# Products of value and output weights kept in DRAM in the first half of a latent attention, and loaded by GpSimd's queue in the second half

## The reference

```python
ctx_c = jnp.einsum('bhsl,bld->bhsd', attn, kv_r)          # probabilities by latent rows, 128 wide
ctx_lat = jnp.einsum('bhsd,hkd->bhsk', ctx_c, w_kc_kv)    # value weights of each of 16 heads
ctx = ctx_lat.transpose(0, 2, 1, 3).reshape(Bv, Sv, H * K)
return ctx @ Wo.T                                         # output weights
# outside:  x = x + jnp.tanh(g_xattn[0]) * that
```

```python
scale = jnp.mean(jnp.abs(w)) + EPS
wq = jnp.clip(jnp.round(w / scale), -1.0, 1.0)
```

## Time and profile before

| | us |
|---|---|
| median of three runs (2047.39 to 2053.69) | 2050.95 |
| the profiled execution's own time | 2053.51 |
| its span | 2051.8 |
| TensorE busy | 1848.8 (90%) |
| VectorE busy | 1403.8 (68%) |
| ScalarE busy | 975.6 (48%) |
| GpSimd busy | 680.5 (33%) |

### The profile page before, as it was taken

How to read it: one execution, slowest core, us unless ns; L and a number is a source line. 1 busy time by engine, 2 the same in 40 slices (tenths; PEclk the granted TensorE clock), 3 DMA queues, 4 the chain that set the end, 5 groups by cost and what they waited for, 6 DMA issues and landing times. The chain is left out here.

```text
span 2051.8 us, 31294 instructions
## 1 busy us (share of the span) xinstructions
PE 1848.8 (90%) x11258; PEld 1452.6 (71%) x11258; DVE 1403.8 (68%) x2821; ACT 975.6 (48%) x2042; POOL 680.5 (33%) x628
## 2 busy tenths in 40 slices
PE   4899999999999899998978997999758899999996
PEld 4677887777877677766754444666537889999996
DVE  5776677777678777788767883766636436666664
ACT  3444444433444344443445654555343236666663
POOL 4332122333523312233100131332221554665653
PEclk9999999999999999999989997999879999999999
DMA  5022201220311322122133111000040447877873
GB/s 201 16 84 81 83 23 61 84 88 3 114 38 35 126 92 75 33 80 96 39 125 151 46 38 32 1 1 1 1 160 23 150 89 211 243 242 228 241 240 76
DMA packets 52397, 192.38 MB, mean 94 GB/s; under 512 B 7678, under 2 KB 11902, under 8 KB 41494
## 3 DMA queue, kind: packets, MB, share of 16 engines
q1 hardware_dynamic: 40550, 167.01, 23.1%
q0 software_dynamic: 11408, 23.37, 6.2%
q10 hardware_dynamic: 288, 0.00, 0.0%
HBM read 156.99 MB, written 33.36 MB: 93 GB/s over the span
## 5 line engine op out<-in xcount | busy, mean ns | idle before, releaser
L363 POOL TENSOR_TENSOR la_q_roped<-la_q_roped 128x400 f32<-128x400 f32 x128 | 139.4, 1111 | 685.8 <-DVE la_q_roped L819 685.8
L722 ACT ACTIVATE la_probs<-banks,la_minus_max 100x361 f32<-100x361 f32 x256 | 144.7, 565 | 197.3 <-DVE la_minus_max L909 197.3
L819 DVE TENSOR_TENSOR la_q_roped<-banks,la_rope_q 128x400 f32<-128x400 f32 x384 | 196.8, 564 | 26.2 <-PE banks L490 16.5
L2069 DVE TENSOR_TENSOR ex_weights_low<-ex_raw_weights,ex_weights_high 128x2048 fp32r<-128x2048 f32 x60 | 137.6, 2293 | 54.9 <-ACT ex_weights_high L1964 52.1
L527 PEld LDWEIGHTS banks<-identity,la_probs 100*121 100x121 f32 x768 | 113.3, 185 | 73.4 <-DVE la_probs L916 48.0
L916 DVE TENSOR_SCALAR la_probs<-la_probs,la_rsum 100x361 f32<-100x361 f32 x256 | 154.5, 603 | 9.1
L538 PE MATMUL banks<-la_probs_t,la_kv_rows 121*128 121x200 f32 x768 | 151.4, 333 | 0.0
L527 PE MATMUL banks<-identity,la_probs 100*121 100x100 f32 x768 | 126.3, 273 | 23.3 <-DVE la_probs L916 20.1
L909 DVE TENSOR_REDUCE la_minus_max<-banks 100x1 f32<-100x361 f32 x256 | 134.8, 527 | 17.1 <-PE banks L518 10.3
L2336 POOL TENSOR_TENSOR ex_g_low<-ex_g,ex_g_high 128x256 fp32r<-128x256 f32 (+1 forms) x104 | 86.7, 950 | 177.4 <-ACT ex_g_high L2008 176.9
L1964 ACT CAST ex_weights_high<-ex_raw_weights 128x2048 fp32r<-128x2048 f32 x60 | 114.1, 1902 | 42.2 <-PE banks L2417 33.9
(11 more groups left out here) (335 smaller groups left out, 5300.7 us busy)
## 6 DMA issues: line engine op xcount, KB each, us to landing
ex_raw_weights<-w_exp SPq DMA_DIRECT2D x60, 1024.0 KB
la_weights<-w_pack SPq DMA_DIRECT2D x15, 1856.0 KB, 7.7
la_kv_turned<-w_ffn SPq DMA_DIRECT2D x30, 384.0 KB
la_rope_k<-w_ffn SPq DMA_DIRECT2D x30, 384.0 KB
qf_sign_weights<-ffn_signs SPq DMA_DIRECT2D x3, 2048.0 KB, 10.0
ffn_signs<-la_ffn_signs SPq DMA_DIRECT2D x30, 192.0 KB, 2.1
residual<-x SPq DMA_DIRECT2D x2, 2048.0 KB, 14.9
out<-ex_block_out POOLq DMA_DIRECT2D x13, 256.0 KB, 4.3
```

The source lines that it names most:

```text
L363: pool.tensor_tensor(roped[:, h, 0, c, :], roped[:, h, 0, c, :], roped[:, h, 1, 1 - c, :], ALU.add).then_inc(b_add, 1)
L722: act.activation(prob[:, s % 4, 0:L], ps[0:S, s % 2, 0:L], ACT.Exp, bias=nmax[:, s % 4:s % 4 + 1], accum_out=sums[:, s % 4:s % 4 + 1]).the ...
L819: dve.tensor_tensor(roped[:, h, v, c, :].rearrange("p (b s) -> p b s", b=GB), ps[:, B_BANKS[k % 2], 0:NT].rearrange("p (b s) -> p b s", b=GB),
L2069: dve.tensor_tensor(wl[:, m, :], raw[:, m, :], wh[:, m, :].bitcast(F32), ALU.subtract).then_inc(w_low[m], 1)
```

## The change

In the first half, SyncE stores `mh` and `ml` of each pass to a DRAM tensor (`keep`, 512 KB each). In the second half, `wout` on TensorE, `wout_high` on ScalarE and `wout_low` on VectorE are left out; GpSimd's queue loads the two matrices instead (`bring`) once the last `out` of the pass before is done, and the first `out` of a pass waits for them.

```diff
@@ latent_attention
+    kept_m = nc.dram_tensor("wout_parts", (PAIRS, 2, DC, 2 * D), F32).ap()
@@ SyncE
+                def keep(n):
+                    sp.wait_ge(m_low, 2 * n + 2)
+                    for i, m in enumerate((mh, ml)):
+                        sp.dma_start(kept_m[n, i], m[:].rearrange("p h d -> p (h d)").bitcast(F32)).then_inc(m_out, 16)
+
                 for n in range(2, RUNS + 1):
+                    if n <= PAIRS + 1:
+                        keep(n - 2)
                     refill_sums(n - 1)
                     refill_signs(n - 2, slice(3, None))
@@ GpSimd
+                def bring(n):
+                    pool.wait_ge(m_out, 32 * PAIRS)
+                    pool.wait_ge(o_psum, n * HB)
+                    for i, m in enumerate((mh, ml)):
+                        pool.dma_start(m[:].rearrange("p h d -> p (h d)"),
+                                       kept_m[n - PAIRS, i].bitcast(F32R)).then_inc(m_in, 16)
@@
                     if starts_half(n):
                         rotate(1, range(HB))
+                    if n >= PAIRS:
+                        bring(n)
                     for u in range(UNITS):
                         partners(n, u)
@@ TensorE, mix and out
-                    else:
+                    elif n < PAIRS:
                         pe.wait_ge(m_low, n * 2 + 1)
@@
-                    if b == 0:
+                    if b == 0 and n < PAIRS:
                         pe.wait_ge(m_low, n * 2 + 2)
+                    elif b == 0:
+                        pe.wait_ge(m_in, 32 * (n - PAIRS + 1))
@@ TensorE, pair
-                    wout(n, 0)
+                    if n < PAIRS:
+                        wout(n, 0)
                     absorb(n, 0)
                     widen(n, 3, 0)
-                    wout(n, 1)
+                    if n < PAIRS:
+                        wout(n, 1)
@@ ScalarE
                     act.wait_ge(m_psum, n * 2 + h + 1)
+                    if n:
+                        act.wait_ge(m_out, 32 * n)
@@ ScalarE, pair
-                    wout_high(n, 0)
+                    if n < PAIRS:
+                        wout_high(n, 0)
@@
-                        if s == 0:
+                        if s == 0 and n < PAIRS:
                             wout_high(n, 1)
@@ VectorE, pair
-                        if s in (MIX - 2, MIX - 1):
+                        if s in (MIX - 2, MIX - 1) and n < PAIRS:
                             wout_low(n, s - MIX + 2)
```

More of the change, by code:

```diff
@@ L212, in latent_attention @@
         m_psum, m_high, m_low = sem("wout_psum"), sem("wout_high"), sem("wout_low")
+        m_out, m_in = sem("wout_stored"), sem("wout_loaded")
         a_psum, a_high, a_low = sem("q_psum"), sem("q_high"), sem("q_low")
```

## The result

The changed kernel takes 2057.15 us (median of 7 runs, 2054.03 to 2059.57) against 2048.79 us for the kernel before in the same runs: 8.4 us more by the medians. The ratio of the means is 1.0035, with a 95% interval of 1.0024 to 1.0046, which is 7.2 us (4.9 to 9.4). The profiled execution has a span of 2055.3 us.

What follows compares the result with a forecast made beforehand. TensorE is busiest, but VectorE bounds the first slots of a pass. Gain -8.0, delay +12.0 and clock +5.1 sum to +9.1 us; on the runs' median of 2050.95 that gives 2060 us, range 2043 to 2070.

Steps and rivals of the forecast that it cites:

- The gain: Work removed in passes 8 to 15: 1.3 us in pass 8, 0.6 in seven others, 2.5 at low clock; 8.0 together.
- low-clock part: Head part at 1.20 GHz: VectorE's longer wait at qk_low gains 0.5 us more in five passes, 2.5 us.
- Rival (b): Passes 8 to 15: TensorE's removed matmuls count whole, 15 us, delay 12, clock holds; 2048 us; chance 0.10.
- The step that decided it: First slots: softmax scaling L916, started earlier, still waits for the same split end, so VectorE's 1.4 us are mostly given back.
- The stores and GpSimd's issues hidden: First half's sixteen stores and GpSimd's two issues per second-half pass: counted as nothing; an issue takes 1.03 us.
- The delay: Starts of passes 10 to 14: loads make the first signs' store late by 2.5 us each, 12.0 us in all.
- straight to TensorE: Second chunk's signs: VectorE's delay passes directly to TensorE, which waits at widen(n, 2, 1) already.
- (a): Second half: GpSimd's loads don't delay SyncE's; only the gain stays, 2043 to 2046 us; chance 0.22.
- (c): Second half: slower transfers in the shared DMA engines, 4.3 us per pass; 2070 us; chance 0.11.
- How the store is late: Pass starts with weights in flight: weights land in about 10 us instead of 7.7, the signs' store over 2 us late.
- The clock: Passes 11, 12 and 14: TensorE idles 3.8 us at once, new clock drops of 1.7 us each, 5.1 us.
- Cost in all: Second half: 12.0 us for the late store of signs plus 5.1 us for new clock drops.

Runs made afterwards that it cites:

- e1: Changed kernel without GpSimd's loads, the second half using pass 7's matrices throughout; 2043.42 us, 0.9969 of the kernel before.
- e2: Changed kernel with GpSimd's two loads behind the last partners of the pass instead of before the first; 2050.47 us, 1.0008 of the kernel before.
- e6: Kernel before with only the first half's stores and ScalarE's wait for them added; 2049.24 us, 0.9993 of the kernel before.
- e7: Kernel before with the stores and GpSimd's loads at the pass's start added, nothing removed; 2063.85 us, 1.0074 of the kernel before.
- e3: Changed kernel with two buffers for signs and a weights load shorter by 256 KB; 2039.04 us, 0.9953 of the kernel before.
- e4: Changed kernel with the weights load shorter by 640 of 1856 KB in passes 8 to 15; 2048.18 us, 0.9984 of the kernel before.
- e11: Changed kernel with loads before the last partners, weights load without value and output columns, two sign buffers; 2037.03 us, 0.9935 of the kernel before.

## Why the prediction was right

- **Direction and size.** Forecast 2060 and +9.1 us, measured 2057.15 and +8.4. The kernel before had a median of 2048.8 in these runs, 2.2 below the one that the sum was added to; on that base the forecast is 2058. By the ratio of the means the change costs 7.2 us. In the two profiles passes 8 to 15 together grow by 8.5 us; what lies before and behind them is 2.2 and 2.8 us shorter, in kernels that differ there by the stores at most.
- **The gain**, forecast 5.5 us without the low-clock part and 8.0 with it: e1 measured 6.4; in its profile the clock is low in the head part of pass 10 only. Passes 8, 9 and 15 of the changed kernel gained 1.5, 0.7 and 0.6, forecast 1.3, 0.6 and 0.6. The 2.5 us for passes with a low clock no run shows by itself. Rival (b), TensorE's removed time in full, falls: 15 us lie outside e1's interval. The step that decided it, that L916 ends with the same instruction of `split` though it starts earlier, is seen in e1's rows; e2 shows it from the other side, where a `split` 1.1 us later makes the scaling 1.1 us longer.
- **The stores and GpSimd's issues hidden**: e6 shows no effect of the stores; GpSimd's issues took 0.55 us each rather than 1.03, and had room in this place. The 1.03 us was a wrong reading: the DMAs of the earlier trace rows add into `out` (`accum_op=ALU.add`), and are not plain ones. That the price of an issue in another place can be a microsecond a pass was not in the prediction.
- **The delay.** Forecast 2.5 us per pass, 12.0 in all. VectorE's wait at the second chunk grew by 3.9 in pass 10, 3.0 in pass 11, 2.7 in pass 12 (3.02 after 0.32), 1.6 in pass 13, and by 3.2 in pass 14: 14.4, or 2.9 a pass. The prediction let it go "straight to TensorE". TensorE's idle time at `widen(n, 2, 1)` grew by 3.9, 2.3, 2.3, 0.8 and 2.5, which is 11.7: in four of the five passes the writing of the signs took 0.4 to 0.7 us less. The 12.0 is so near to 11.7 because one error makes up for the other, and that is luck. That it is the loads is shown by e7, that it is nearly all this wait by e3. Rivals (a) and (c) fall with it, as neither 0 nor 4.3 us per pass came out.
- **How the store is late** was put wrongly in one point: the weights were to land in about 10 us and the store right behind. They landed in 8.7 in pass 11, at 754.3, and the store only at 756.8, when the DMA traffic was running out (a share of 0.34 in the window from 756). That the bytes in flight set the delay was right (e4), the order in which they finish was not. In which order the engines served the two queues was not tried.
- **The clock.** Three new drops were counted, in passes 11, 12 and 14, 1.7 us each. The changed kernel's profile has the drop in all three, and in passes 10 and 13 as before. But they are not all of one length. In the 9.5 us behind TensorE's wait the mean clock was 0.76, 0.82, 0.70, 0.82 and 0.82 in passes 10 to 14; measured against full clock, that is 6.9 us more lost than before, where 5.1 was forecast: 2.9 in pass 12, and 0.6 in pass 10, where nothing new was counted. In e7's profile the drop is missing in passes 12 to 14 behind waits of 2 to 2.8 us, so no such figure holds for every execution. No experiment separated the clock's share. An estimate comes from the granted clock on record for each run: the span times what the mean clock lacks to 1 is 76 us over seven runs of the changed kernel, and 68 to 69 over 49 runs of the kernel before; e7 has 74, e1 and e3 have 68. By this some 7 us of low clock go with the loads, and go away with the second buffer; part of it lies in the wait itself, where it costs nothing.
- **Cost in all**: forecast 17.1 us, e7 measured 15.1 (11 to 19). In the profile of the change the wait and the clock come to 18.6. Passes 10 to 14 are together 11.3 us longer than before, forecast 11.6. Mechanism and direction were right; that the total is nearer than its terms is in part luck.

## What to carry to other kernels

Before a transfer is put at a place where "the queue is free", look at what else the DMA engines have in flight there, and which engine waits for a small store or load with no margin: here a store of 128 to 192 KB decided what 1 MB of loads cost, whose own reader had 30 us to spare. Against the kernel before, a second buffer of 1.5 KB per partition brought 9.6 us (6.6 to 12.5), and moving the loads into a gap of their issuer 7.8 (5.1 to 10.5), which these runs can't tell apart; both together, with a shorter load of weights, brought 13.3. Of the 1.5 us a pass taken from VectorE beside GpSimd's `split`, 1.2 were taken back by instructions that ended with GpSimd's: look who stands beside removed work before pricing it.

## What was not expected of the hardware

- GpSimd's DMA issue takes 0.55 us for 512 KB here, against 1.03 us for the adding DMA into `out` of 256 KB.
- A softmax scaling of VectorE beside `split` took 2.58 us instead of 1.45 when `split` started 1.1 us later; each of these ended about 0.2 us behind an instruction of GpSimd.
- TensorE's clock fell behind an idle time of 2.00 us in one profile and held behind 3.24 us in another.
- The first 550 us of the program differ by over 3 us between profiled executions of kernels with the same first half (549.5 in e11 to 552.9 in e2).
